# Moving GpSimd's weight splits and one VectorE normalisation near the end of the attention loop of a decoder layer

## The reference, cut to what matters

```python
x = x + attn(layernorm(x))                    # self attention
x = x + xattn(layernorm(x), ctx, bias)        # 16 x 1500 keys, softmax per head
xf = layernorm(x)
scores = softmax(xf @ Wg);  weights, indices = top_k(scores, 4)
y = sum over e of swiglu(xf[tok], W1[e], W2[e], W3[e]) * w     # first 448 pairs of e
x = x + y + swiglu(xf, Ws1, Ws2, Ws3)
```

## Time and profile before

| | |
|---|---|
| Median of 3 runs | 479.01 us (478.52 to 479.05) |
| Profiled execution | 479.18 us, span 477.4 us |
| Mean granted TensorE clock | 0.942 of full speed |
| Busy share of the span | PE 89%, DVE 73%, ACT 67%, POOL 62% |
| Chain that ended last | PE 72%, DVE 11%, ACT 5%, POOL 5%, DMA 3%, issue 2% |

### The profile page before, as it was taken

One profiled execution on the slowest core, in us unless ns is written; L12 is line 12 of the kernel. 1 busy time (PEld: TensorE's weight loads), 2 busy tenths in 40 slices (PEclk: granted clock), 3 DMA queues, 4 the chain that ended last, 5 costly groups with the idle time before them and its releaser, 6 DMA issues.

```text
span 477.4 us, 16298 instructions
## 1 busy us (share of the span) xinstructions
PE 423.2 (89%) x6928; PEld 292.1 (61%) x6928; DVE 348.6 (73%) x544; ACT 319.3 (67%) x675; POOL 297.9 (62%) x249
## 2 busy tenths in 40 slices
PE   3338968798999999999999999999989699989996
PEld 2125747265676776766766767767766486555674
DVE  7364537987778877778877778777778744869796
ACT  6415622466887788888788887878877497464563
POOL 7789467989686685685685765857837461544100
PEclk9856986699999999999999999999999799999999
DMA  6477338556858867568559489295343000000000
GB/s 156 148 134 137 113 86 224 128 151 135 193 155 131 182 155 140 163 143 172 149 107 209 133 121 172 103 114 157 123 96 85 2 2 3 1 0 1 25 1 18
DMA packets 78120, 53.30 MB, mean 112 GB/s; under 512 B 62968, under 2 KB 69216, under 8 KB 78048
## 3 DMA queue, kind: packets, MB, share of 16 engines
q1 hardware_dynamic: 76136, 50.88, 48.0%
q0 software_dynamic: 1248, 0.85, 0.7%
q10 hardware_dynamic: 664, 0.52, 0.4%
HBM read 17.05 MB, written 0.46 MB: 37 GB/s over the span
## 4 chain that ended last, share of the span: by engine, by line
PE 72%; DVE 11%; ACT 5%; POOL 5%; DMA 3%; issue 2%; ACTq 1%; SPq 1%; DVEq 0%; POOLq 0%
PE ps L1042 18%; PE ps L867 13%; PE ps L1018 6%; PE ps L375 4%; PE ps L377 4%; PE ps L376 4%; PE ps L870 4%; DVE mx L1625 3%; PE ps L1166 3%; PE ps L795 2%; PE ps L798 2%; PE ps L796 2%; DVE mself L1485 2%; PE ps L877 2%; PE ps L900 2%
## 5 line engine op out<-in xcount | busy, mean ns | idle before, releaser
L1625 DVE TENSOR_REDUCE mx<-ps 120x2 f32<-120x1000 f32 x192 | 221.1, 1195 | 58.4 <-PE ps L1018 58.4
L1319 ACT ACTIVATE p<-ps 125x448 f32<-125x448 f32 x288 | 141.6, 549 | 19.3 <-PE ps L1042 15.7
L1042 PE MATMUL ps<-qall,ks 128*125 128x224 f16 x768 | 127.8, 272 | 5.9 <-DMA qall<-mrow 1.9
L1042 PEld LDWEIGHTS ps<-qall,ks 128*125 128x125 f16 x768 | 76.7, 137 | 44.0 <-issue 19.1
L625 POOL TENSOR_TENSOR k<-k,zero 128x500 f16<-128x500 f32 x48 | 49.8, 1037 | 66.7 <-ACT k L1245 52.2
L867 PE MATMUL ps<-p,v 125*27 125x168 f32 x1152 | 65.3, 312 | 0.1
L629 POOL TENSOR_TENSOR k<-k 128x500 f16<-128x500 f32 x48 | 54.4, 1134 | 3.8
L1319 ACT ACTIVATE wnat<-ps 125x448 f32<-125x448 f32 x96 | 47.1, 542 | 9.8 <-PE ps L1042 9.8
L611 POOL TENSOR_TENSOR ch<-ctx,ch 128x1536 f16<-128x1536 f32 x16 | 49.8, 3110 | 1.5 <-DMA ct<-ch 0.3
L1018 PE MATMUL ps<-ks,qall 31*56 31x500 f16 x768 | 43.7, 404 | 3.9 <-DVE mx L1625 3.3
L601 POOL TENSOR_TENSOR ch<-ctx,zero 128x1536 f16<-128x1536 f32 x16 | 44.0, 2748 | 2.5 <-issue 2.4
(11 more groups left out here) (198 smaller groups left out, 771.7 us busy)
## 6 DMA issues: line engine op xcount, KB each, us to landing
ks<-k SPq DMA_DIRECT2D x48, 375.0 KB
ctx<-in_ctx SPq DMA_DIRECT2D x16, 672.0 KB
ctx<-in_L_ffn_W SPq DMA_DIRECT2D x48, 64.0 KB, 2.2
ks<-brow SPq DMA_DIRECT2D x32, 46.9 KB
ctx<-in_ctx SPq DMA_DIRECT2D x16, 78.0 KB
ct<-ch SPq DMA_TRANSPOSE x32, 6.3
qall<-q POOLq DMA_DIRECT2D x12, 42.0 KB, 3.2
xs<-in_x SPq DMA_DIRECT2D x1, 448.0 KB, 4.0
```

The lines of the kernel that those rows point to most:

```text
L1042: last = mm(stb[score_bank(r, c, s, half)][0:KP, 224 * (g % 2):224 * (g % 2) + 224], ks[c % 3][:, g, KP * s:KP * s + KP], qall[:, g, :, 3 ...
L1319: A(p[s % 4][0:KP, 448 * half:448 * half + 448], stb[score_bank(r, c, s, half)][0:KP, 0:448], ACT.Exp, scale=SCALE).then_inc(exp_done, 1)
L1625: V.tensor_reduce(mx[:, h:h + 2, k // 2], mxb[0:120, 2 * pair:2 * pair + 2, 0:CH], axis=AX.X, op=ALU.max).then_inc(mx_read, 1)
```

## The change

GpSimd: units 8 and 9 are split before the four instructions that make the routing constants and before `send_maxima(13)`, not behind them. `rstd_of(2, 0)` now follows unit 13 (before: unit 12). Behind it stands a new wait, for `xn_ok` at 18, which is reached when `norm_apply(2, 0)` has written its four tiles. Then comes unit 14, then `send_maxima(14)` and the pair selector, and units 15 and 16 after it (before: only unit 16).

VectorE: `norm_apply(2, 0)` moves in iteration 14 from the end of step 1 to the end of step 2, behind that step's `normalize` and `take_round`.

```diff
                         split_unit(u)
+            for u in range(2 * NW, 2 * NW + 2):
+                split_unit(u)
             memset(ones_h[:], 1.0)
...
             send_maxima(B - 3)
-            for u in range(2 * NW, 3 * NW + 1):
+            for u in range(2 * NW + 2, 3 * NW + 2):
                 split_unit(u)
             rstd_of(2, 0)
-            for u in range(3 * NW + 1, 4 * NW):
-                split_unit(u)
+            pool.wait_ge(xn_ok, 2 * TT + TILES[0][1])
+            split_unit(3 * NW + 2)
             send_maxima(B - 2)
...
-            split_unit(NP)
+            for u in range(3 * NW + 3, UNITS):
+                split_unit(u)
...
-                    if i == B - 2 and d == 1:
+                    if i == B - 2 and d == 2:
                         norm_apply(2, 0)
```

## The result

| | before | changed |
|---|---|---|
| Median | 478.95 us (6 runs, 478.2 to 479.25) | 474.88 us (6 runs, 473.44 to 477.11) |
| Ratio | | 0.9923, 95% interval 0.9897 to 0.995 |
| Profiled execution | 479.18 us, span 477.4 | 475.05 us, span 473.2 |
| Busy PE, DVE, ACT, POOL | 89%, 73%, 67%, 62% | 89%, 73%, 67%, 63% |

A forecast was written before the change was run, and what follows sets the result against it. In iteration 14 TensorE waits 2.92 us for `tok`, behind `xn` slowed by GpSimd's splits, then runs at half clock. A gain of 3.85 us less 0.65 us gives -3.2 us: 475.9 us, range 475.0 to 476.7.

The forecast's parts named there:

- What bounds the kernel: Iteration 14: `xn` and `tok` slowed by GpSimd's splits, TensorE waiting 2.92 us, then half speed for 6.8 us.
- Step 1: Iteration 14, VectorE: `tok` before `xn` ends TensorE's wait for `tok`; transposes gain 2.87 us, with new waits of 0.5 and 1.3.
- Step 2: GpSimd: units 8 and 9 fit before `send_maxima(13)`, and holding unit 14 keeps GpSimd still during `xn`; cost 0.
- Step 3: Iteration 14, transposes to scores of tile 8: the clock holds, 1.0 of a 3.85 us gain; odds five to two.
- the clock falls all the same: Rival: clock falls at iteration 14's new waits, before dense work, costing 1.7 us, giving 477.5 us; chance 0.22.
- Step 4: Iteration 15's routing: VectorE's cast and `tok` meet GpSimd's later splits, losing 0.65 us, bounds 0 and 1.3.
- Sum: Whole kernel: -3.85 + 0.65 = -3.2 us, giving 475.9 us.
- the slow `xn`: Rival: iteration 14's four `xn` were not slow because of GpSimd and still take 3.35 us; 478.4 us, chance 0.06.
- the long low stretch: Rival: clock falls at 377.5 and stays low into iteration 15, costing 4.95 us; 480.8 us, chance 0.06.

The follow-up runs named there:

- e2: Changed kernel with `norm_apply(2, 0)` back at the end of step 1, so GpSimd's edit alone: 475.11 us, ratio 0.9936 to the kernel before.
- e6: Kernel before plus 16 unread products on TensorE ahead of "tr" in iteration 14, in its wait for `tok`: 475.89 us, ratio 0.997 to the kernel before.
- e5: Changed kernel without GpSimd's new wait for `xn_ok`, unit 14 split right behind the power: 475.02 us, ratio 0.9942 to the kernel before.
- e4: The changed kernel itself, unaltered, timed and profiled again as a control: 474.19 us, ratio 0.9907 to the kernel before.
- e1: Kernel before with VectorE's edit alone, GpSimd's order as it was: 474.93 us, ratio 0.9926 to the kernel before.
- e10: Changed kernel with pair selector early, iteration 14's transposes a step later, and 8 unread TensorE products at the start of iteration 0: 472.75 us, ratio 0.9896 to before.
- e3: Changed kernel with the pair selector's memset and first select moved behind the power, second select before units 15 and 16: 473.70 us, ratio 0.9898 to before.

## Why the prediction was right, point by point

**What bounds the kernel**: right. e2 shows it by itself: with GpSimd still, `xn` falls from 3.43 to 1.10 us and nearly the whole gain is there, the clock's part included, which held in e2.

**Step 1, VectorE's order**: right in mechanism. `tok` was ready 4.96 us behind the addition, 4.99 forecast, and TensorE's wait for it went. The term that was mis-sized is `xn`: 1.11 us where I took 1.4, four times the median of single rows. Back to back one takes 0.28. The transposes came 8.77 us behind the addition, 11.96 before: 3.19 gained, 2.87 forecast; 0.37 of it is what the low clock had cost the kernel before ahead of its transposes (e6). The new waits are 0.48 (forecast 0.5) and 0.94 (1.3). What I didn't see is how much the two edits overlap. Both take `xn` away from the splits. GpSimd's alone gives 3.09 of 3.64 us, so VectorE's adds 0.55; VectorE's alone reaches the same median.

**Step 2, GpSimd's order**: right. Unit 9 was split by 354.5; counted back from the addition that is 11.3 us, 11.4 forecast. The sends weren't held, and nothing waited for them. The hold that I counted on to protect `xn` protects `tok`, by 0.4 us (e5): unit 14 alone would have been over before `xn`.

**Step 3, the clock**: right for the profiled execution, and near in size: from the transposes to the scores of tile 8 it took 1.57 us, not 2.74, a gain of 1.17 where I had 1.0. e6 shows separately that the low clock cost the kernel before 1.37 us. The rival "the clock falls all the same" was half right: it fell in two of the changed kernel's three profiles. But I had priced it at 1.7 us, in front of dense work; it fell ahead of the two waits and cost nothing. So the term came out whether the clock held or not, and my reason for it, that it holds, was wrong in two of the three: that much is luck. Nor does busy time, by which I argued, tell when it falls: in e4 TensorE had been busy for 2.54 of the 3.41 us ahead of the fall (367.96 to 371.37), while the profiled execution of the changed kernel went through 3.40 us with 1.98 busy (371.9 to 375.3) at full clock. What a fall costs where less hides it, e1 and e10 show: 1.56 and 0.86 us.

**Step 4, the routing**: right in mechanism; that it is right to the hundredth, between bounds of 0 and 1.3, is luck. At the scores of tile 8 the gain is 14.70 - 10.34 = 4.36 us, and at the last "tr" of the loop 25.57 - 21.86 = 3.71: 0.65 lost, in TensorE's wait that grew from 0.33 to 0.99. L1505 took 0.75 and the cast 0.34, 0.50 and 0.16 more than alone. Unit 16's end and the routing both came 0.5 us earlier than forecast, since both follow the scores of tile 8 (the send of the maxima begins 0.61 behind them before and after), so the distance between them was as forecast. Step 2's 377.3 to 377.5 for that send does not agree with the 377.8 of step 4; the 0.61 bears out step 4. By the Trainium skill, "SBUF — State Buffer", "Who interferes with whom", a product with two SBUF inputs contends with a GpSimd instruction that reads SBUF, and a cast can; the trace agrees on both. But the cast's wait did not bring the loss near the 1.0 that I had worked out from the page: `tok` ends just behind unit 16 (387.41 and 387.30) which I read as unit 16's end setting its own; no run has the one wait without the other. e3 gained 1.04 us by giving back both and L1575.

**Sum**: 3.64 us on the profile, 3.2 forecast. The missing 0.4 is `xn` (0.3) and the clock (0.2), within the 0.1 to which the spans are read: at the last "tr" the gain is 3.71. The rivals of the slow `xn` and of the long low stretch did not occur.

## What to carry to other kernels

- When a short instruction takes the time of another engine's instruction beside it, look at where it ends: if it ends just behind the other's end, move one of the two, and check what the moved one meets in its new place. Here the splits cost 0.65 us a whole iteration later, until GpSimd's memset and select went into the time in which it only waited.
- Here a low clock cost time only where TensorE's work ended last. Waits for other engines hid it, and a change that removed these waits uncovered it (0 in the changed kernel, 0.86 us in e10).
- Where whole executions spread by more than the effect, compare a stretch of the profile between two fixed instructions; here it repeated within 0.04 us over five profiles of the changed kernel and its two variants with added products.

## What the runs showed that I had not expected

- GpSimd's memset, which writes only, did not slow VectorE's two-input product beside it: in e3 the memset ran from 369.04 to 370.83 and L1509, from 370.35, took 0.25 us. The Trainium skill, "SBUF — State Buffer", "Who interferes with whom", says so of a GpSimd instruction that only writes SBUF.
- At one place of one program the clock falls in some executions and not in others: in the changed kernel's three profiles twice at 371 us, once not at all. The addition in iteration 14 comes anywhere from 364.65 to 369.08 us; about 1.4 us of that is a fall of the clock at 120 us, the rest arises earlier, and its cause stays open.
